# A perceiver block on one core: the first cross-attention tile in another order, and its scores over 256 columns in the later tiles

## The reference, cut to what matters

```python
def _L0_xattn_ref(hidden_states, encoder_hidden_states, Wq, Wk, Wv, Wo, bo):
    q = hidden_states @ Wq
    k = encoder_hidden_states @ Wk
    v = encoder_hidden_states @ Wv
    ...
    scores = jnp.einsum('bhsd,bhkd->bhsk', q, k) * scale
    probs = jax.nn.softmax(scores, axis=-1)
    out = jnp.einsum('bhsk,bhkd->bhsd', probs, v)
    out = out.transpose(0, 2, 1, 3).reshape(B, S, H * Dh)
    return out @ Wo + bo
...
x = x + _L0_xattn_ref(_layernorm(x, axis=-1), ctx_768, ...)
x = x + _L0_attn_ref(_layernorm(x, axis=-1), ...)
x = x + _L0_ffn_ref(_layernorm(x, axis=-1), ...)
```

## Time and profile before

| | us |
|---|---|
| time, median of three runs (lowest to highest) | 1615.67 (1614.93 to 1616.33) |
| the profiled execution: its own time | 1616.33 |
| its span, first to last instruction | 1614.5 |
| TensorE busy in the span | 1556.0 (96%) |
| VectorE busy | 1071.8 (66%) |
| ScalarE busy | 734.9 (46%) |
| GpSimd busy | 367.8 (23%) |
| mean granted clock of TensorE, share of full speed | 0.988 |

### The profile page before, as it was taken

The page is one execution under the profiler, slowest core; times in us unless marked ns, Lnnn a source line. Parts: engine busy times, 40 slices in busy tenths (PEclk is TensorE's granted clock), DMA queues, the critical chain, the costliest instruction groups (busy, mean ns, idle before and its releaser), DMA issues.

```text
span 1614.5 us, 36223 instructions
## 1 busy us (share of the span) xinstructions
PE 1556.0 (96%) x13768; PEld 1293.2 (80%) x13778; DVE 1071.8 (66%) x2314; ACT 734.9 (46%) x1587; POOL 367.8 (23%) x223
## 2 busy tenths in 40 slices
PE   7999878999999999999999999999999999996989
PEld 6888767889888898889988898878878878784444
DVE  7776656676667666676677766657555565555788
ACT  5544544555455554555455554433222222223755
POOL 0000134434434344434434344400000000000000
PEclk9999999999999999999999999999999999998999
DMA  6898853422343133322343143250310302232022
GB/s 239 320 363 333 321 223 111 148 67 112 135 135 131 60 137 129 140 73 105 135 135 133 59 136 121 80 196 22 106 67 28 126 34 72 99 136 116 0 104 105
DMA packets 80042, 213.56 MB, mean 132 GB/s; under 512 B 5776, under 2 KB 31824, under 8 KB 77136
## 3 DMA queue, kind: packets, MB, share of 16 engines
q1 hardware_dynamic: 79952, 212.27, 36.4%
HBM read 141.86 MB, written 70.39 MB: 131 GB/s over the span
## 4 chain that ended last, share of the span: by engine, by line
PE 73%; issue 12%; DVE 8%; ACT 4%; DMA 3%; SPq 0%; DVEq 0%; POOL 0%; ACTq 0%; POOLq 0%
PE psum_o L666 12%; PE psum_s L643 7%; PE psum_q L643 6%; PE psum_o L1373 6%; PE psum_q L1373 6%; PE psum_o L681 5%; PE psum_q L1413 5%; PE psum_t L1442 5%; PE psum_o L535 5%; PE psum_t L654 2%; DVE qk L1039 2%; PE psum_t L614 2%; PE psum_s L1400 1%; ACT qk L786 1%; PE psum_t L567 1%
## 5 line engine op out<-in xcount | busy, mean ns | idle before, releaser
L666 PE MATMUL psum_o<-pT,c_nat 128*128 128x512 f32 x1152 | 309.9, 406 | 6.3 <-issue 4.0
L1223 POOL TENSOR_TENSOR c_nat<-c_raw,constants 128x768 fp32r<-128x768 f32 x64 | 95.4, 1490 | 629.5 <-PE psum_o L666 456.3
L666 PEld LDWEIGHTS psum_o<-pT,c_nat 128*128 128x128 f32 x1152 | 204.8, 190 | 41.7 <-DVE pT L904 5.3
L1105 DVE TENSOR_SCALAR oT<-psum_o,c_last 128x512 f32<-128x512 f32 x192 | 143.3, 746 | 67.1 <-PE psum_o L666 67.1
L643 PE MATMUL psum_s<-cT,qk 128*128 128x258 f32 x1152 | 170.2, 290 | 5.9 <-DVE qk L1039 1.9
L643 PEld LDWEIGHTS psum_s<-cT,qk 128*128 128x128 f32 x1152 | 152.9, 191 | 15.6 <-DVE cT L904 6.2
L643 PE MATMUL psum_q<-cT,qk 128*128 128x258 f32 x1152 | 155.0, 286 | 0.0
L845 ACT ACTIVATE probs<-psum_s,nmax 128x257 f32<-128x257 f32 x128 | 61.2, 478 | 201.8 <-DVE nmax L1120 201.8
L643 PEld LDWEIGHTS psum_q<-cT,qk 128*128 128x128 f32 x1152 | 144.2, 190 | 5.1 <-issue 5.1
L904 DVE TENSOR_TENSOR pT<-psum_t,pT 128x512 fp32r<-128x512 f32 x128 | 87.7, 686 | 74.1 <-ACT pT L744 74.1
L1208 POOL TENSOR_TENSOR c_raw<-c_raw,last_row 128x768 f32<-128x768 f32 x64 | 118.2, 1846 | 29.1 <-DMA last_row<-in_ctx_dram 29.1
(11 more groups left out here) (272 smaller groups left out, 3109.4 us busy)
## 6 DMA issues: line engine op xcount, KB each, us to landing
qk_by_tile<-staged SPq DMA_DIRECT2D x32, 1536.0 KB, 9.8
raw<-qk_by_tile SPq DMA_DIRECT2D x16, 3072.0 KB, 12.4
c_raw<-in_ctx_dram SPq DMA_DIRECT2D x64, 384.0 KB, 3.2
last_row<-in_ctx_dram SPq DMA_DIRECT2D x64, 192.0 KB, 4.1
out_dram<-x_out SPq DMA_DIRECT2D x32, 256.0 KB, 2.0
x_res<-in_x_dram SPq DMA_DIRECT2D x16, 256.0 KB, 2.7
x_in<-out_dram SPq DMA_DIRECT2D x4, 1024.0 KB, 8.1
x_res<-out_dram SPq DMA_DIRECT2D x16, 256.0 KB, 3.3
```

The costliest lines, as they stand in the source:

```text
L666: i = pe.matmul(ps[:], c_nat[(b - 1) % 2][:, part, k, m * P:(m + 1) * P], pT[:, moving, k, :], start=(k, part, moving) == (0, 0, 0), stop= ...
L1105: nc.vector.tensor_scalar(oT[:, m, :, (b - 1) % 4, :], ps[:].rearrange("p (s q) -> p s q", q=SQ), c_last[:, (b - 1) % 2, m:m + 1], None, A ...
```

## The change

Nine edits, all in the cross attention.

- At the end of the projections the last chunk of context 0 is turned behind head pair 4 and not ahead of it. ScalarE makes the high query part 0 behind pair 4 and part 1 behind pair 6 (before: 0 behind pair 6, 1 behind pair 7).
- The low query parts 0 and 1 of tile 0 are made by GpSimd (`pool_qk_low`); VectorE waits for both and makes 2 and 3, each ahead of a row maximum.
- In stage 0 of the first tile context 1 is turned between the scores: chunks 0 and 1 behind row group 1, chunk 2 behind row group 2. ScalarE's and VectorE's instructions of that stage are written out anew.
- Context 2 is loaded behind the store of pair 4, when context 0 has been turned.
- Behind the last store SP issues Wo, context 3, the next tile's queries, Wv, the bias and x, and then contexts 4 and 5.
- Wo has a semaphore of its own and is split in quarters of 128 x 1024. ScalarE makes them at the end of stage 1, within stage 2, at the ends of stages 2 and 3; VectorE one at the end of stage 1, two at the end of stage 2, one at the end of stage 3.
- GpSimd subtracts the last row from context 1 ahead of splitting context 0.
- GpSimd splits context 0 as soon as group 3 of x has been turned, and context 1 once all four query parts are split.
- In the 15 tiles behind the first, scores have 256 columns, but for the last row group of stage 0, whose bank Wo's product uses in between.

```diff
@@ project_units (the places of the moved chunk alone)
-                    u += [(("CT", "start", c), ("t0", "t1")[c % 2]) for c in range(3)]
+                    u += [(("CT", "start", c), ("t0", "t1")[c]) for c in range(2)]
...
@@ pe_project_all
-                    for c in range(KC):
+                    for c in range(2):
                         pe_ctxT_chunk(pe, project(("CT", "start", c)), c_raw[0], c)
                 for j in range(4, 8):
                     pe_group_qk(pe, s, j)
+                    if (s, j) == (GROUPS - 1, 4):
+                        pe_ctxT_chunk(pe, project(("CT", "start", 2)), c_raw[0], 2)
@@ pe_scores
+            keys = SKP if section == "first" or (b, rg) == (0, 3) else 2 * P
...
-                    m = pe.matmul(ps[:, 0:SKP], qk[:, part, rg, c, b, :], cT[b % 2][:, moving, c, :],
+                    m = pe.matmul(ps[:, 0:keys], qk[:, part, rg, c, b, :], cT[b % 2][:, moving, c, 0:keys],
@@ pe_cross_tile
+                if not before:
+                    pe_ctxT(pe, t, b, section, (0, 1))
                 pe_scores(pe, t, b, 2, section)
...
+                if not before:
+                    pe_ctxT(pe, t, b, section, (2,))
                 pe_scores(pe, t, b, 3, section)
@@ act_project_all
-                    if s == GROUPS - 1 and j >= 6:
-                        act_qk_high(act, 0, j - 6)
+                    if (s, j) == (GROUPS - 1, 4):
+                        act_start_context(act, 2)
+                    if s == GROUPS - 1 and j in (4, 6):
+                        act_qk_high(act, 0, j // 2 - 2)
@@
+        def act_wo_high(act, k):
+            act.wait_ge(s_wo, 16)
+            nc.scalar.activation(wo_quarter(wo_high, k), wo_quarter(wo_raw, k), ACT.Copy).then_inc(s_wohi, 1)
@@ act_cross_tile
+            if not begun:
+                exp(0, 0)
+                exp(0, 1)
+                ctxT(0, 0)
+                ctxT(0, 1)
+                scale(0, 0)
+                ctxT(0, 2)
+                exp(0, 2)
+                scale(0, 1)
+                exp(0, 3)
+                act_last_scalars(act, t, 0, section)
...
+                if b == 2 and not begun:
+                    act_wo_high(act, 1)
...
-                if section == "first" and b in (1, 2):
-                    act_wo_high(act, b - 1)
+                if b < 3 and not begun:
+                    act_wo_high(act, 2 * (b - 1))
+            if not begun:
+                act_wo_high(act, 3)
@@ dve_cross_tile
-                if section == "first" and b >= 2:
-                    dve_wo_low(dve, b - 2)
+                if b < 3 and not begun:
+                    dve_wo_low(dve, 2 * (b - 1))
+                    if b == 2:
+                        dve_wo_low(dve, 1)
+                if b == 3 and not begun:
+                    dve_wo_low(dve, 3)
@@
+        def pool_qk_low(pool, t, rg):
+
+            pool.wait_ge(s_qhi, 4 * t + (rg + 1))
+            part = [qk[:, i, rg, :, :, :].rearrange("p c b (h q) -> p h (c b) q", h=4) for i in range(2)]
+            nc.gpsimd.tensor_tensor(part[1], raw[:, :, rg, :].rearrange("p h (a q) -> p h a q", q=SQ),
+                                    part[0].bitcast(F32), ALU.subtract).then_inc(s_qlo, 1)
@@ sp_project_all
+                    if (s, j) == (GROUPS - 1, 4):
+                        full(sp, project(("CT", "start", 2)))
+                        sp.wait_ge(s_nat, 1)
+                        load_ctx(sp, 0, 2)
...
             for i in range(4):
                 sp.wait_ge(s_staged[i], 32 * GROUPS)
+            sp.dma_start(wo_raw[:], Wo.rearrange("(k p) n -> p k n", p=P)).then_inc(s_wo, 16)
+            full(sp, U1(("CT", 0, 2), 0, "first"))
+            sp.wait_ge(s_nat, 2)
+            load_ctx(sp, 0, 3)
+            load_qk(sp, 0, 1)
             sp.dma_start(wv[:], Wv.rearrange("(k p) n -> p k n", p=P)).then_inc(s_wvo, 16)
-            sp.dma_start(wo_raw[:], Wo.rearrange("(k p) n -> p k n", p=P)).then_inc(s_wvo, 16)
             sp.dma_start(bo_all[:], bo.rearrange("(a n) -> a n", a=1).to_broadcast([P, D])).then_inc(s_wvo, 16)
             sp.dma_start(x_res[:], rows(x_rows, 0)).then_inc(s_xres, 16)
+            for b in range(2, 4):
+                sp.wait_ge(s_nat, b + 1)
+                load_ctx(sp, 0, b + 2)
```

131 lines of the change are left out of this document (76 added, 55 removed).

## The result

| | median us | runs (lowest to highest) |
|---|---|---|
| before | 1616.0 | 4 (1614.93 to 1617.12) |
| changed | 1607.15 | 4 (1606.35 to 1608.8) |

The ratio is 0.9943, with a 95% interval of 0.9931 to 0.9955: the changed kernel is 8.85 us faster. The forecast was 14.8 us faster, at 1600.9 us. The time lies in the range, but near its upper end of 1608 us, and for a reason that the text ahead does not have. The profiled execution of the changed kernel took 1608.8 us (span 1607.0), the slowest of the four.

A forecast was written before the change was run, and what follows sets the result against it. TensorE bounds the steady tiles; in the first tile it waits for VectorE, GpSimd and a late load. Terms 1.45 + 3.5 + 6.5 + 1.6 + 1.7 = 14.75 us gave a median of 1600.9 us, range 1597 to 1608 us.

The forecast's parts named there:

- term 1: Start of first tile: query parts on GpSimd save 0.9 us, context turned between the scores 0.55 us; 1.45 us.
- term 2: First tile's second half: Wo's quarters wait for Wo alone, each low part 1.3 us on VectorE; 3.5 us saved.
- term 5: Scores of the 15 later tiles: 256 instead of 258 columns shorten 2025 TensorE products; 1.7 us saved.
- Term 3: First tile's loads: context 3's last row lands sooner, so TensorE's wait of 6.50 us goes; 6.5 us saved.
- B: Experiments' rival, Wo's low quarters on VectorE: slow for their place or SBUF traffic; 1605 us or more with memsets.
- C: Experiments' rival, Wo's load: its late landing is the loss; with memsets context 3's first product shifts under 1 us.
- term 4: First tile, products behind the removed c_raw wait: no longer at the lower clock of 1.2 GHz; 1.6 us saved.
- land with the queue: First tile: context's load shares DMA engines with loads queued behind, landing near 222 us; 1611.0 us; chance 0.08.
- the first rival: Start: GpSimd's query parts are dear; 7.5 us each gives 1607.6 us, 9.4 us gives 1611.4 us; chance 0.12.

The follow-up runs named there:

- the first run: Changed kernel with each quarter of Wo's low part made a VectorE memset that reads nothing; 1601.56 us, ratio 0.9918 to the kernel before.
- the run with the turns first: Changed kernel; in the first tile's context 3 VectorE makes turned context 4's low parts ahead of the next tile's query parts 1 to 3; 1613.74 us.

## Why the prediction had the side and not the size

The gains by its steps, from the table of the first section (the two profiles of the changed kernel):

| step | forecast | changed | second profile |
|---|---|---|---|
| term 1, start | 1.45 | 1.02 | 1.05 |
| term 2, quarter of context 2 | 2.0 | -0.25 | 1.65 |
| terms 3 and 4, loads and clock | 8.1 | 7.52 | 8.68 |
| term 2, quarters of context 3 | 0.25 | -1.71 | -1.71 |
| term 2, second tile | 1.25 | 0.16 | 0.12 |
| term 5, columns | 1.7 | 0.83 | 0.96 |
| sum | 14.75 | 7.57 | 10.75 |

**Term 2 is the step that failed**: 3.5 us forecast, -1.8 and 0.1 us in the two profiles. Its mechanism was right as far as it went: the wait for Wv and the bias is gone, and what counts is how long VectorE is late for its row maximum. Its price was wrong: "a quarter's low part on VectorE takes 1.3 us: half of 2.56 to 2.99 us". Those two rows already held a wait for a GpSimd instruction, which does not halve with the work. A half is 2.15 us of work and 0.4 to 0.85 us of waiting; a quarter is 1.1 us of work and up to 1.85 us of waiting, and there are four. The hint lay in rows that the forecast shows, 2.99 us in the earlier trace rows and 3.77 us in the earlier trace rows, at the same moment. Term 3 even uses the second one, and lets GpSimd stand still beside VectorE's quarter; that VectorE stands still for GpSimd as well enters no term. The waits that the forecast would leave at 0.3, 1.4 and 0.3 us (that is 2.0) were 2.56, 3.40 and 0 us, with a later chunk wait of 2.64 us where 1.21 stood before.

Shown: the exclusion itself, both ways (quarters that read nothing are not held up, quarters on GpSimd hold VectorE's query parts up), that halves are 3 us better than quarters, and that quarters placed clear of it give 1602.28 us, 1.4 us from the forecast time. As causes of the loss, rivals B and C of the experiments fell with the first run. Of C this remains: the forecast has no DMA waited for, but Wo was issued at 200.17 us, where it had 198 to 199.5, landed 9.4 us later, and ScalarE waited 1.50 us for it. VectorE's 0.85 us ahead of the first quarter come from there, and they put the quarter just behind the start of GpSimd's low part.

**Terms 3 and 4 were right.** The wait for `c_raw` went, and the products behind it run at 2.4 GHz for the most part (clock 0.97 from 219.80 to 223.20 us): from the turned context to the first scores of context 3 it is 3.69 us (219.52 to 223.21) where it was 5.77. So term 4 alone is 2.1 us, and term 3 is 5.4 us in this profile. The last row of context 3 landed at 211.8 us, later than the 206 to 208 us of the forecast, but GpSimd was busy until 212.52 us anyway. TensorE came late to the transposes in this profile; in the second one it came at 215.83 us, where the forecast has 215.7, and GpSimd was done at 214.67. Undone, the order of the loads costs the whole gain. In the first profile a stretch at 1.2 GHz remains behind the wait of 2.56 us (clock 0.50 from 216.80 to 219.80 us), which is why the window of context 2 has 0.88.

**Term 1** has the right price for GpSimd (3.5 us) and in the two profiles of the changed kernel nearly the right size, but not the right source. Of it 0.9 us were to come from the parts; VectorE does end the last one about 0.9 us sooner, but the run with VectorE's parts gives only 0.15 us of the gain to GpSimd. VectorE waited 2.77 us for GpSimd at the start, so that little was won by having two engines. In three of eleven profiles the whole term is lost to a scaling that stands behind GpSimd, a wait that the forecast does not have. The Trainium skill, "GPSIMD Engine Reference", section "Engine selection", which the forecast weighed, puts such work on VectorE; the 3.5 against 1.7 us a part and the small gain agree with it.

**Term 5** was sized at twice its worth: 0.8 us, not 1.7. The price per column was the slope between products of 258 and 512 columns; two columns off 258 give 0.4 ns a product (0.75 us in 14 tiles of 135 products), where that slope gives 0.85. The lower bound of 0 was named, and the truth lies in the middle.

**The rivals.** GpSimd's parts were not dear, the context did not land with the queue, and no rival named VectorE waiting for GpSimd at Wo. The range reached 1608 us because of the first rival and held the time by its width, not by its reasons.

The Trainium skill states what was missed, on its page "SBUF — State Buffer", section "Who interferes with whom": a VectorE instruction with two inputs in SBUF contends with a GpSimd instruction that reads SBUF, the first to issue has the shared ports for the whole instruction, and the other "fully blocks". The traces agree: 2.92 us = 1.84 us of GpSimd's 1.85 and 1.08 us of work, and 912 ns for a memset that reads nothing. The same section counts `tensor_scalar` in a two-port mode among those that contend. No row shows which mode the scalings by `rden` run in; their 0.61 us alone and 2.26 us beside GpSimd's quarter agree.

## What to carry to other kernels

Where VectorE and GpSimd are both at work, list the instructions of VectorE with two inputs in SBUF and of GpSimd near each other in time, and count for each meeting up to the whole of the other's instruction; a duration read at such a place is work and waiting, and only the work scales with the size. Cutting such an instruction in pieces buys a shorter piece and sells more meetings: halves beat quarters here by 3 us. What helps is to put the work on whichever engine has the gap while the other reads PSUM, and a load that lands with the queue behind it is worth checking before any of this: with its place in the queue undone, all of the measured gain was gone.

## What the runs showed of the hardware

- Ten or twenty nanoseconds decide who stands still. In the changed kernel the first quarter began 0.01 us behind GpSimd's instruction and took 2.92 us. In the run with the turns first, the same up to there, it began at 210.31 us, 0.02 us ahead of GpSimd's, and took 1.23 us, while GpSimd's took 2.91. Two profiles of one kernel then differ by 1.9 us at the first product of context 2 (41.13 and 39.20 us). The spread of a kernel's executions does not tell of it: on one chip the changed kernel's ran from 1604.93 to 1609.89 us and those of the version with three quarters on GpSimd from 1601.58 to 1602.84, but those of the kernel before from 1615.01 to 1620.65.
- The time in which an instruction stands still for the other engine is counted in its own duration, as busy time: the row of 2.92 us shows no idle time of that kind, and the waits of TensorE behind it name "issue". In a table of waits this loss is not to be seen; it shows as one form with several durations (1496/2392/2920 ns over the changed kernel's four quarters, 912 ns four times for the memset).
- A scaling by `rden`, with a single tensor of 256 columns to read, is held up as well: 0.35 us where it began ahead of GpSimd's subtraction, 1.86 us where it began 0.11 us behind.
- Two engines that each have several such instructions in a row take turns: 9.15 us for 5.1 us of work on VectorE, and 3.22 and 3.33 us for 1.85 us each on GpSimd, in one stretch.
- A quarter of Wo's low part takes 2.40 us on GpSimd and, alone, 1.21 us on VectorE, a query part 3.5 and 1.74 us: twice as long, at both sizes.
